# One attention loop over both batches, with the second batch's projection cut in pieces inside it

## What is computed

```python
xn = layernorm(x, ln_x_g, ln_x_b)               # context, 77 rows
ln = layernorm(latents, ln_l_g, ln_l_b)         # layernorm(x), 1024 rows
q = ln @ W_q
kv = jnp.concatenate([xn @ W_kv, ln @ W_kv], axis=1)
k, v = (kv[..., :INNER], kv[..., INNER:])
q, k, v = (to_heads(q), to_heads(k), to_heads(v))
qn = rmsnorm(q, q_gamma) * SCALE
kn = rmsnorm(k, k_gamma)
sim = jnp.einsum('bhid,bhjd->bhij', qn, kn)
sim = jnp.where(full_mask[:, None, None, :], sim, neg)
attn = jax.nn.softmax(sim, axis=-1)
out = jnp.einsum('bhij,bhjd->bhid', attn, v)
return out @ W_out + b_out
...
x = x + jnp.tanh(g_xattn[0]) * L0_xattn(ctx, layernorm(x), mask, ...)
```

## Time and profile before

| | us |
|---|---|
| median of 3 runs | 959.72 |
| lowest and highest | 959.28, 959.78 |
| the profiled execution | 959.11 |
| its span, first to last instruction | 957.4 |
| mean granted TensorE clock | 0.92 of 2.4 GHz |
| PE, DVE, ACT, POOL busy | 850.4, 588.6, 306.5, 366.0 |
| first projection and attention of batch 0 | about 49 to 243 |
| projection and attention of batch 1 | 243.5 to 436 |

### The profile page before, as it was taken

How to read it: one execution, slowest core, us unless ns; L and a number is a source line. 1 busy time by engine, 2 the same in 40 slices (tenths; PEclk the granted TensorE clock), 3 DMA queues, 4 the chain that set the end, 5 groups by cost and what they waited for, 6 DMA issues and landing times.

```text
span 957.4 us, 13235 instructions
## 1 busy us (share of the span) xinstructions
PE 850.4 (89%) x4334; PEld 630.9 (66%) x4335; DVE 588.6 (61%) x1122; ACT 306.5 (32%) x656; POOL 366.0 (38%) x371
## 2 busy tenths in 40 slices
PE   6887699998785899987999879999999689999995
PEld 5454455554454555545888767777777589999995
DVE  4957656553476456645998868889887723333331
ACT  4556133333261323334344122222222012232230
POOL 4255544233156533444443424444442322232221
PEclk9999589798696889996999989999999889999998
DMA  9380000000000000007200090000000165555520
GB/s 303 121 308 31 1 0 1 1 1 1 0 1 0 1 1 0 1 1 271 77 0 1 5 346 13 11 12 11 12 11 17 50 224 193 183 170 178 192 83 3
DMA packets 32134, 67.87 MB, mean 71 GB/s; under 512 B 3161, under 2 KB 23095, under 8 KB 30999
## 3 DMA queue, kind: packets, MB, share of 16 engines
q1 hardware_dynamic: 28887, 56.63, 17.2%
q0 software_dynamic: 2624, 10.49, 3.5%
q10 hardware_dynamic: 578, 0.18, 0.1%
HBM read 55.20 MB, written 13.01 MB: 71 GB/s over the span
## 4 chain that ended last, share of the span: by engine, by line
PE 69%; DVE 17%; issue 6%; ACT 5%; DMA 2%; POOL 1%; DVEq 0%; SPq 0%; ACTq 0%; POOLq 0%
PE PS L1809 8%; PE PS L1797 8%; PE PS L643 7%; PE PS L1200 6%; PE PS L1182 6%; PE PS L1026 4%; PE PS L634 4%; PE PS L614 4%; DVE NM L713 4%; PE PS L635 3%; PE PS L667 2%; PE PS L579 2%; DVE hL L1123 2%; PE PS L1184 2%; PE PS L1010 2%
## 5 line engine op out<-in xcount | busy, mean ns | idle before, releaser
L821 ACT ACTIVATE EX<-PS 128x512 f32<-128x512 f32 x144 | 79.2, 594 | 169.0 <-PE PS L635 166.4
L713 DVE TENSOR_REDUCE NM<-PS 128x1 fp32r<-128x1101 f32 x64 | 82.7, 1302 | 69.6 <-PE PS L614 69.6
L804 POOL TENSOR_TENSOR sumP<-sumP,EX 128x1024 f32<-128x1024 f32 x32 | 75.8, 2369 | 37.7 <-ACT EX L821 36.5
L1797 PEld LDWEIGHTS PS<-xeT,w 128*128 128x128 f32 x736 | 85.6, 192 | 3.9 <-DMA w<-in_L_ffn_W 1.7
L1797 PE MATMUL PS<-xeT,w 128*128 128x128 f32 x736 | 86.1, 275 | 2.4 <-DMA w<-in_L_ffn_W 1.4
L1809 PE MATMUL PS<-w,heT 128*128 x368 | 83.3, 379 | 1.3 <-DVE oe L1739 1.3
L1809 PEld LDWEIGHTS PS<-w,heT 128*128 128x128 f32 x368 | 68.1, 190 | 10.0 <-issue 1.7
L1200 PE MATMUL PS<-vw,pcT 128*128 128x256 f32 (+1 forms) x320 | 73.1, 383 | 1.2 <-ACT pcT L1392 1.2
L643 PE MATMUL PS<-EX,V 128*64 128x512 f32 (+1 forms) x288 | 73.3, 626 | 0.0
L1836 POOL DMA_INDIRECT out<-oe,target x23 | 23.3, 1011 | 126.2 <-DVE oe L1739 126.2
L634 PE MATMUL PS<-QA,KA 100*128 100x512 f32 x144 | 68.9, 478 | 1.2 <-ACT EX L821 1.2
(11 more groups left out here) (266 smaller groups left out, 1708.3 us busy)
## 6 DMA issues: line engine op xcount, KB each, us to landing
w<-in_L_ffn_W SPq DMA_DIRECT2D x31, 1024.0 KB, 5.6
vw_rows<-vwn SPq DMA_DIRECT2D x2, 1232.0 KB
kwH_rows<-kwH SPq DMA_DIRECT2D x1, 2464.0 KB
kwL_rows<-kwL SPq DMA_DIRECT2D x1, 2464.0 KB
kwH<-kwH_rows POOLq DMA_DIRECT2D x1, 2464.0 KB, 9.9
kwL<-kwL_rows POOLq DMA_DIRECT2D x1, 2464.0 KB, 15.0
vw<-vw_rows SPq DMA_DIRECT2D x2, 1152.0 KB, 7.3
XR<-in_x SPq DMA_DIRECT2D x4, 512.0 KB, 14.1
```

Of the source, the lines that this page charges most:

```text
L713: dve.tensor_reduce(NM[:, n % 2, t // GT, SHIFT + t % GT:SHIFT + t % GT + 1], PSf[:, 512 * at:512 * at + KEYS], AX.X, ALU.max, negate=True ...
L804: pool.tensor_tensor(sumP[:], before, EX[:, (KT * n + c) % EB, :, :], ALU.add).then_inc(pool_summed, 1)
L821: act.activation(EX[0:r, k % EB, i, :], PS[0:r, ST_AT + i, :], ACT.Exp).then_inc(exp_done, 1)
L1797: last = pe.matmul(PS[:, 1 + 2 * p + c // 4, c % 4 * P:c % 4 * P + P], w1[:, u, k, c * P:c * P + P], xeT[:, p, k, :], start=k == 0, stop=k ...
```

## The change

Projection and attention of batch 0 and of batch 1 become one: pe_project(0), then one loop over n = 0 to 7. The order of pairs within a batch changes from (queries 0: heads 01, 23; queries 1: heads 01, 23) to heads 01 with both halves of the queries, then heads 23, so that the keys and values of heads 01 are done with after n = 1.

Batch 1's projection is cut into 18 half pieces: (v, i) is item i for the heads 2v and 2v + 1. An item is one product of 384 columns (queries, keys and values of two heads) into one bank, and a turn of 4 heads into one bank. Two tables say at which step of which pair: items and turns of v = 0 stand in n = 1 and 2, of v = 1 in n = 3 and 4. Rows are normalized and turned in five units of two tiles (NORM_AT, ROWS_AT) in n = 0 to 2. Each piece overwrites keys, values and queries of heads that batch 0 no longer reads.

Row scores have two products (1024 keys, banks 0 and 1); those of 77 context keys for 4 tiles go together into one spare bank (ctx_scores), with a maximum of their own (ctx_max) and a minimum of the negated two (both_max). Banks 2, 6 and 7 are spare banks, given in turn to every use (context scores, shifts, sums, outputs, rows, turned heads, items) in the order of the list spare_uses. PE waits (open_bank) until the reader of the use three before has counted up that bank's semaphore; project_out no longer waits for reciprocals or for the adds of its other half by themselves.

In the projection that remains (batch 0), queries and keys are turned, copied and given their low parts with a count for each. Some semaphores are merged, and pool_bias and pool_wproj move into the loop (n = 3 and 4 at c = 7; after n = 5).

```diff
-    CHUNKS = ((0, 512), (512, 1024), (1024, KPAD))
-    MAX_AT, ST_AT, PV_AT, OUT_AT = 0, 3, 5, 6
+    CHUNKS = ((0, 512), (512, 1024))
+    MAX_AT, ST_AT, PV_AT = 0, 3, 5
+    SPARE = (2, 6, 7)
-    heads_of = lambda j: (2 * (j % 2), 2 * (j % 2) + 1)
+    group_of = lambda n: n % 2
+    heads_of = lambda n: (2 * (n // 2 % 2), 2 * (n // 2 % 2) + 1)
+    FIRST_AT = {2: (0,), 4: (1,), 6: (2,), 8: (3,)}
+    SECOND_AT = {0: (4,), 2: (5,), 3: (6,), 5: (7,), 6: (8,)}
+    FIRST_TURNS = {4: (0,), 6: (1,), 8: (2,)}
+    SECOND_TURNS = {1: (3,), 2: (4,), 4: (5,), 5: (6,), 7: (7,), 8: (8,)}
+    ROWS_AT = {(0, 7): 0, (1, 1): 1, (1, 5): 2, (1, 8): 3, (2, 4): 4}
+    NORM_AT = {(0, 5): 0, (0, 8): 1, (1, 4): 2, (1, 7): 3, (2, 1): 4}
...
+    def open_bank(pe, *use):
+        k = order_of[use]
+        if k >= 3:
+            pe.wait_ge(bank_free[k % 3], k // 3)
+        return SPARE[k % 3]
...
+        def item(v, i):
+            k0 = open_bank(pe, "item", v, i)
+            wait_read(pe, "rows", i // 2, 0)
+            for k in range(KC):
+                last = pe.matmul(PS[:, k0, 0:3 * P].rearrange("p (t n) -> p t n", t=3), lnT2[:, k, i * P:i * P + P],
+                                 wqkv[:, k, :].rearrange("p (t n) -> p t n", t=3)[:, :, v * P:v * P + P],
+                                 start=k == 0, stop=k == KC - 1)
+            last.then_inc(qkv_done, 1)
+
+        def keys_there(n):
+            if n % 2 == 0 and n >= PAIRS0:
+                pe.wait_ge(high_ready, keys_of(n // 2 - 1, LAST))
+                wait_read(pe, "heads", n // 2 - 2, LAST)
+                pe.wait_ge(v_ready, unit_item(n // 2 - 2, LAST) + 1)
+                pe.wait_ge(keys_ready, unit_item(n // 2 - 2, LAST) + 1)
...
+        for n in range(PP):
             for c in range(KT):
-                key_scores(j, c)
+                key_scores(n, c)
+                if n + 1 < PP:
+                    if c == 0:
+                        keys_there(n + 1)
                     if c < 2 * GT:
+                        pe.wait_ge(max_ready, 2 * GT * (n + 1) + c)
+                        row_scores(n + 1, c, MAX_AT)
+                    if c in (3, 7):
+                        ctx_scores(n + 1, c // 4)
+                    if c in (5, 8):
+                        turn_shift(n + 1, (c - 5) // 3)
...
+                if (n, c) in ROWS_AT:
+                    turn_rows(ROWS_AT[n, c])
+                for v, i in turns_at(n, c):
+                    turn_heads(v, i)
+                for v, i in items_at(n, c):
+                    item(v, i)
                 for done in CHUNK_OF_STEP.get(c, ()):
-                    values(j, done)
+                    values(n, done)
...
+    def dve_attend(dve):
...
+                for v, i in turns_at(*step_before(n, c)):
+                    low_parts_of(v, i)
+                for v, i in items_at(*step_before(n, c)):
+                    scale_heads(v, i)
+                if n + 1 < PP and c < 2 * GT:
+                    row_max(n + 1, c, MAX_AT)
+                if n + 1 < PP and c in (3, 7):
+                    ctx_max(n + 1, c // 4)
+                    both_max(n + 1, c // 4)
...
+                for v, i in items_at(n, c):
+                    square_sums(v, i)
+            sum_rest(n)
...
+    def pool_attend(pool):
...
+                for v, i in turns_at(n, c):
+                    w, h0 = (P if i < LAST else C + 1), 2 * v
+                    pool.wait_ge(high_ready, keys_of(1 + v, i))
+                    pool.tensor_copy(KA[0:E0, h0:h0 + 2, i * P:i * P + w],
+                                     KB[0:E0, h0:h0 + 2, i * P:i * P + w].bitcast(F32)).then_inc(keys_ready, 1)
+                for v, i in items_at(n, c):
+                    pool.wait_ge(rms_mean, unit_item(v, i) + 1)
+                    pool.tensor_tensor(rrms[:, i % 2, 0:4], rms2[:, i % 2, 0:4], minus_half[:, 0:4], ALU.pow) \
+                        .then_inc(rrms_ready, 1)
...
-        for b in range(B):
-            pe_project(pe, b)
-            pe_attend(pe, b)
+        pe_project(pe, 0)
+        pe_attend(pe)
```

The halves in the projection of batch 0:

```diff
-            if i >= 1:
-                pe.wait_ge(low_ready, item(i))
-            for h in range(0 if i < LAST else H0, 2 * H0):
-                last = pe.transpose(PS[:, 6 + h // H0, (h % H0) * P:(h % H0) * P + P],
-                                    qk2[:, i % 2, h, :, :].rearrange("p a e -> p (a e)"), ident[:])
-            last.then_inc(qkT_done, 1)
+            for part in range(0 if i < LAST else 1, 2):
+                if i >= 1:
+                    pe.wait_ge(low_ready, (queries_of, keys_of)[part](b, i - 1))
+                for h in range(part * H0, part * H0 + H0):
+                    last = pe.transpose(PS[:, 6 + part, (h % H0) * P:(h % H0) * P + P],
+                                        qk2[:, i % 2, h, :, :].rearrange("p a e -> p (a e)"), ident[:])
+                last.then_inc(qkT_done, 1)
```

469 lines of the change are left out of this document (301 added, 168 removed).

## The result

The changed kernel takes 933.4 us (median of four runs, 931.87 to 937.26) where the kernel before took 959.5 (957.66 to 959.78): a ratio of 0.9738, 95% interval 0.9706 to 0.977. It is 2.6% faster, 13.4 us above the forecast point of 920.0, inside the range of 898 to 952 and 1.4 us beyond the band of 912 to 932 that the forecast gave itself. The profiled run took 933.5 us with a span of 931.1.

The account below looks back on a forecast made before the run. PE (TensorE) was taken to bound the loop, a chain through all engines the 81 us between; 959.1 - 5 - 81.4 + 46.5 + 0.2 = 919.4, with 0.6 for the median 920.0 us; range 898 to 952.

Parts of the forecast that it names:

- the mechanism and its main terms: 81.4 us between the loops go; pieces moved into n = 1 to 4 add 46.5; first projection -5.
- the signs that the prediction named: No stretch between batches; four pairs 38-42 us, granted 0.85 or more; n = 5, 6 at 30-33.
- the waits cancel: Pairs with pieces: 2 us of PE waits removed and 2.2 us added per pair, so no net cost.
- base: Pairs n = 1 to 4 before adding pieces, each taken at 31.0 us, the mean of four earlier pairs.
- keys_there: Starts of n = 3 and 5: PE waits before row scores 0 for the last low part; some 1.5 us, twice.
- split: First projection, queries and keys handled as halves: steps of 4.63 us become about 4.0; -5 us, bounds 0 and -8.
- wait (1): Pair start: row maximum 0 queued on VectorE behind sum_rest, low parts and scaling; about 1 us added.
- (2): Added wait for keys_there at n = 3 and 5, before row scores 0; some 1.5 us, twice.
- the slower rival: Pairs with pieces: holes between pieces and transposes keep the clock at its low level; +56, 976 us; chance 0.13.
- Today the low level follows the sums: Loop before the change: low clock comes after one-column sums, about 6 us of each pair, costing 3 us.
- bias and wp cost nothing: Both moved into the loop on POOL, where it idles at the end of a pair; no cost.
- open_bank: After project_out, a piece waits for the bank add_out reads; about 0.8 us once or twice a pair.

Follow-up runs that it names:

- the doubled product: Each piece's product made twice into its bank, against the changed kernel with the last low part ahead of sum_rest; 948.7 us, ratio 0.9908.
- the kernel without pieces: Changed kernel with batch 1's pieces left out, its pairs reading batch 0's projection; 879.2 us.
- the kernel with short sums: Pairs 1 to 6: 16 one-column sum products made one of eight columns, against the change with last low part ahead of sum_rest; 909.4 us.
- the hole: PE waits for the second adds at step 4 of n = 3 and 5, against the change with last low part ahead of sum_rest; 933.6 us.
- the maximum first: VectorE's row maximum ahead of low parts and scaling, against the change with the last low part ahead of sum_rest; 941.7 us, ratio 0.9836.
- the scaling last: VectorE order low parts, row maximum, scaling, against the change with the last low part ahead of sum_rest; 925.4 us, ratio 0.9655.

## Why the prediction was right, and where it was off

**Right: the mechanism and its main terms.** 81.4 us of poorly filled time went, the pieces' work came back in four pairs, and TensorE is busy for 37.6 to 40.0 us of each 40.0 to 43.2. That a piece's work is not free there is shown by the doubled product (20.0 of 23 us) and by the kernel without pieces (11.9 us a pair). VectorE's load was put at 30.6 us of a pair and measured 26.1 to 32.3; POOL's at 18.3, measured 16.7 to 23.0; neither bounds. ScalarE needed no other table. Row maxima (+0.75), n = 0 (+0.6) and the tail (-1.1) came out within half a microsecond. Of the signs that the prediction named, most came: n = 3 and n = 5 did not, at 43.2 and 36.9 us where it had 38 to 42 and 30 to 33, and n = 3 was granted 0.84 where it had 0.85 or more.

**The failed step: "the waits cancel".** The prediction took 2 us a pair as removed and 2.2 as added. The removed ones were hardly there: by the earlier trace rows TensorE is idle for only 1.1 us in a pair (29.90 less 28.79), and 4.5 us of "waiting" had been worked out from pitches, which a busy TensorE already contains. Added were 2.4 us of idle time a pair beyond the kernel without pieces. In n = 1 to 4 the terms are, for four pairs: base 119.1 against 124 predicted; TensorE's busy time 37.7 more, where 34.0 had been counted (31.2 + 1.6, and 1.2 for context matmuls, which the kernel without pieces has in its base); idle time 9.7 more, where 2.0 stood for keys_there and the other waits were to cancel. Of the busy time's excess 3.4 us are the clock: 23.8 us at the low level against 17.0 without pieces. 166.5 against 160.0: the base was 4.9 too dear and the additions 11.4 too cheap. That the time came within 13.4 us is in part luck: the dear base, and a split worth 2.5 us more than forecast, hid 7.4 us of a miss of about 21. The prediction called this its weakest step.

**keys_there: right place, wrong size.** 2.29 and 2.43 us, not 1.5: two additions of 1.22 and 1.23, and then the mask's copy (0.23) and the low part (0.39) are queued behind one another. Worse, the sum held 2.0 us for it in n = 1 to 4 and nothing for the one in n = 5, a pair that was given 0.3 us. And taking it away gave only 4.7 us, for the row maximum behind the same sum_rest was late next, which the prediction had listed as wait (1) and had not added up with (2).

**The clock.** It is granted at 0.96, 0.96, 0.84 and 0.96 in n = 1 to 4, so the slower rival (0.75 and less) was far off. But the stretches of 13.6 us in n = 3 and 13.7 in n = 5 were in no term. Without pieces the same starts have 3.4 and 6.8 us, and half of the difference is 5.1 and 3.5 us. "Today the low level follows the sums" fits the stretch read for it, and the short ones after; the two long ones begin ahead of the sums, as the wait for the keys ends, so this miss and that of keys_there are not independent. So n = 5, with 36.9 us for 31.5 before, is keys_there (2.4) and the clock (3.5); n = 7, 1.6 us longer, has one stretch of 3.4 us (0.93) where the last pair before had none (1.00). The rule of the Trainium skill ("TensorE: Matmul & The Clock Gate", Part 4) that transposes don't count as work was weighed in the prediction; the pairs with turns beside their products run at 0.96 but for n = 3, and the kernel with short sums keeps every turn and has 6.7 us left of 34.0, so the runs do not bear the rival out.

**The split: under-priced.** -7.5 us, near the bound of -8 and not at -5. The turns of batch 0 start at 67.97, 71.75, 75.52, 79.61 and 83.61 in the kernel after: 3.8 to 4.1 us a step, and 3.8 in the mean with the next two, where the prediction said 4.0. Six steps of 4.63 us became 23.0 us in all, 4.8 less, close to the 4.4 counted. What was too small is the little that was given to the steps at either end: the last took 4.09 us for 5.50, the first 5.33 for 6.10, and the turns began 0.55 earlier, 2.7 us together. Joining the halves gave 8.3 us back in the trace.

**"bias and wp cost nothing": false, though cheap.** The cover was looked for on POOL, where it is. The cost arises on VectorE, whose small operation is held up for 2 us by the bias in n = 4, with TensorE 1.65 us behind it, and for 1.89 us by wp in n = 5, with TensorE 0.45 us behind. Moving the bias gained nothing that can be measured.

**open_bank: right.** Product, turns and project_out wait 4.1, 0.7 and 1.1 us in all, 1.1 at most, where 0.8 us once or twice a pair was forecast.

**Open.** How waits and sums together set the length of the low level: at the start of n = 5 it is 13.6 or 13.7 us in five kernels, 10.2 in three, two stretches with the high level between them in two (6.8 and 6.8 with the hole, 3.4 and 6.8 with the product twice), 6.8 with the maximum first and without pieces, none with short sums; no run takes every wait away and leaves the sums as they are. The 2.1 us after the loop, where nothing was changed. Whether the five kernels with medians from 925.4 to 929.9 differ among themselves: the keys ahead of sum_rest are common to all of them and the only edit whose gain was followed to its waits; each median is 3.5 to 8 us below that of the change, with the scaling last the lowest (925.4).

## What to carry to other kernels

When work of a badly filled stage is moved into a stage that one engine bounds, count all of that engine's work as new time, take only the idle time that the windows show as room, and expect waits and clock on top (here 11.9 us a pair for work that was counted as 8.2). Ask of every wait that an edit removes what stands behind it in the same queue: here the keys, the row maximum and the sums were behind the same two additions, and each reordering handed the wait to the next. Give what frees a shared buffer (the low parts) the first place in a queue; the same edit in the other order cost 13 us.
